# The first wave's four base rows: turned on TensorE, or turned in blocks on VectorE and carried inside SBUF

## What is computed

```
# layer 0, per batch
q, k, v = x @ Wq, x @ Wk, x @ Wv
attn_out = softmax(q k^T / 16) v @ Wp + bp
cms_out  = gelu(attn_out @ cW1 + cb1) @ cW2 + cb2 + one_hot(code)
modifier = gelu(concat(attn_out, cms_out) @ mW1 + mb1) @ mW2 + mb2
x = clip(x + cms_out + modifier, 0, 1)
# layers 1 to 3: adapters, whose weights are picked per batch by role (3 roles)
h = gelu(x @ W_down[role] + b_down[role])
y = x + h @ W_up[role] + b_up[role]
x = (y - mean(y)) * rsqrt(var(y) + 1e-5) * gamma[role] + beta[role]
```

## Time and profile before

| | |
|---|---|
| median of three runs | 352.44 us (352.42 to 353.86) |
| the profiled execution, its own time | 354.08 us |
| its span, first to last instruction | 352.3 us |
| TensorE busy | 341.1 us (97%) |
| VectorE busy | 206.5 us (59%) |
| ScalarE busy | 167.3 us (47%) |
| GpSimd busy | 61.4 us (17%) |
| wave 1's base rows by TensorE (L1569) | four pairs, at 111.9, 115.8, 119.7 and 124.7 us |

### The profile page before, as it was taken

How to read it: one execution, slowest core, us unless ns; L and a number is a source line. 1 busy time by engine, 2 the same in 40 slices (tenths; PEclk the granted TensorE clock), 3 DMA queues, 4 the chain that set the end, 5 groups by cost and what they waited for, 6 DMA issues and landing times.

```text
span 352.3 us, 6682 instructions
## 1 busy us (share of the span) xinstructions
PE 341.1 (97%) x2247; PEld 284.1 (81%) x2247; DVE 206.5 (59%) x493; ACT 167.3 (47%) x331; POOL 61.4 (17%) x96
## 2 busy tenths in 40 slices
PE   6899999999999999999999999999999999999994
PEld 6687687787788888788877777877899999999972
DVE  6048367441452886576554666554689777554576
ACT  3455686463552563544145455343455554543431
POOL 2710060000040110011320111003212125100222
PEclk9899999999999999999999999999999999999998
DMA  6574599468120214234075897303746533288001
GB/s 214 175 254 137 152 139 125 68 139 181 43 60 0 70 39 134 75 90 120 21 245 148 254 309 253 76 31 92 215 151 195 160 113 98 63 281 337 25 2 45
DMA packets 35704, 46.93 MB, mean 133 GB/s; under 512 B 9852, under 2 KB 20406, under 8 KB 35670
## 3 DMA queue, kind: packets, MB, share of 16 engines
q1 hardware_dynamic: 33910, 42.51, 44.9%
q0 software_dynamic: 1392, 3.80, 3.8%
q10 hardware_dynamic: 368, 0.20, 0.2%
HBM read 43.60 MB, written 4.48 MB: 136 GB/s over the span
## 4 chain that ended last, share of the span: by engine, by line
PE 83%; DVE 6%; POOL 3%; ACT 3%; issue 3%; DMA 1%; DVEq 0%; POOLq 0%
PE bank L332 12%; PE bank L334 11%; PE bank L333 11%; PE bank L1499 9%; PE bank L1504 8%; PE bank L1500 8%; PE bank L1546 4%; PE bank L1522 4%; PE bank L1361 2%; PE bank L1403 2%; PE bank L1421 2%; ACT h_full L847 1%; PE bank L1577 1%; ACT h_hi L851 1%; PE bank L1519 1%
## 5 line engine op out<-in xcount | busy, mean ns | idle before, releaser
L847 ACT ACTIVATE h_full<-bank,bias 128x512 f32<-128x512 f32 (+1 forms) x80 | 48.2, 602 | 111.4 <-PE bank L334 101.7
L1082 DVE TENSOR_TENSOR h_lo<-h_full,h_hi 128x512 fp32r<-128x512 f32 (+1 forms) x80 | 46.8, 585 | 60.8 <-ACT h_hi L851 57.4
L767 POOL TENSOR_TENSOR rstd<-moments,minus_half 128x1 f32<-128x1 f32 x39 | 23.4, 600 | 168.6 <-DVE moments L1155 168.5
L851 ACT ACTIVATE h_hi<-h_full 128x512 fp32r<-128x512 f32 (+1 forms) x80 | 43.7, 546 | 2.5
L1140 DVE TENSOR_TENSOR window_y<-bank,window_x 128x256 f32<-128x256 f32 x39 | 16.5, 423 | 37.6 <-PE bank L1522 26.0
L1499 PE MATMUL bank<-h_hi,m_hi 128*128 128x512 f32 (+1 forms) x80 | 30.2, 387 | 0.2
L1499 PE MATMUL bank<-h_hi,c_hi 128*128 128x512 f32 (+1 forms) x80 | 30.1, 385 | 0.2
L332 PE MATMUL bank<-at_hi,c_hi 128*128 128x512 f32 (+1 forms) x80 | 29.3, 367 | 0.0
L332 PE MATMUL bank<-at_hi,m_hi 128*128 128x512 f32 (+1 forms) x80 | 28.7, 359 | 0.0
L334 PE MATMUL bank<-at_lo,c_hi 128*128 128x512 f32 (+1 forms) x80 | 27.8, 348 | 0.0
L333 PE MATMUL bank<-at_hi,c_lo 128*128 128x512 f32 (+1 forms) x80 | 27.8, 347 | 0.0
(11 more groups left out here) (238 smaller groups left out, 729.6 us busy)
## 6 DMA issues: line engine op xcount, KB each, us to landing
adapter_w<-packed_w SPq DMA_DIRECT2D x44, 256.5 KB, 3.4
adapter_rows<-packed_rows SPq DMA_DIRECT2D x36, 256.0 KB, 5.4
stage<-in_L_cond_mW SPq DMA_DIRECT2D x6, 512.0 KB, 4.4
mixed_w<-packed_w SPq DMA_DIRECT2D x8, 256.5 KB, 4.3
stage<-in_L_cond_cW SPq DMA_DIRECT2D x4, 512.0 KB, 5.7
last_w<-packed_w SPq DMA_DIRECT2D x2, 769.5 KB, 6.0
up_bias<-in_L_cond_b_up SPq DMA_DIRECT2D x12, 128.0 KB, 3.7
adapter_rows<-packed_rows SPq DMA_DIRECT2D x24, 64.0 KB
```

The lines of the kernel that those rows point to most:

```text
L767: pool.tensor_tensor(slot.rstd[:, :], slot.moments[:, 1:2], minus_half[:, :], ALU.pow)\
L847: act.activation(h_full[:, n % 2, rows], bank[n % 2][:, rows], ACT.Gelu, bias=bias[:, b:b + 1])\
L851: act.activation(h_hi[:, n % 2, rows], h_full[:, n % 2, rows], ACT.Copy).then_inc(h_hi_ready, 1)
L1082: dve.tensor_tensor(h_lo[:, n % 2, rows], h_full[:, n % 2, rows], h_hi[:, n % 2, rows].bitcast(F32), ALU.subtract).then_inc(h_lo_ready, 1)
```

## The change

Windows 0 to 3 have no "S" use any more: TensorE's eight transposes and VectorE's four additions out of bank 6 go. In their place VectorE turns the 32 x 32 blocks of the window's part of `xT` into `slot.y` (four instructions, windows 0 and 1 behind step H 1 of group 1, windows 2 and 3 behind H 2), SyncE carries them with four transfers for each window from `slot.y` to `slot.x` (sixteen, behind the weights of window 1's layer 1), and VectorE adds `up_bias` to `slot.x` in place, ahead of the addition at L1140. `move_blocks` counts `blocks_turned` four higher, and `row_loads` counts Q = 4 transfers more.

```diff
@@ use numbers of the banks
-                                       [("S", w, 0) for w in starts(wave, spot)] +
+                                       [("S", w, 0) for w in starts(wave, spot) if w not in WAVES[1]] +
@@ row_loads
-            return sum((WIN if v in MIXED else 1) * (2 if n == 0 else 1) for v in range(w % SLOTS, w + 1, SLOTS)
-                       for n in range(LAYERS) if v < w or n <= layer)
+            return Q + sum((WIN if v in MIXED else 1) * (2 if n == 0 else 1) for v in range(w % SLOTS, w + 1, SLOTS)
+                           for n in range(LAYERS) if v < w or n <= layer)
@@ SyncE
-                sp.wait_ge(blocks_turned, n + 1)
+                sp.wait_ge(blocks_turned, len(WAVES[1]) + n + 1)
...
+            def base_rows(w):
+
+                slot = slot_of(w)
+                sp.wait_ge(blocks_turned, w + 1)
+                for m in range(Q):
+                    sp.dma_start(slot.x[:, :].rearrange("p (k m a) -> p m k a", k=VB, m=Q)[:, m, :, :],
+                                 slot.y[quarter(m), :].rearrange("p (i n) -> p i n", i=Q)).then_inc(slot.rows_in, 16)
...
                 window_weights(w, layer)
+                if n == len(WAVES[1]) + 1:
+                    for base in WAVES[1]:
+                        base_rows(base)
@@ VectorE, before: ups
+                    if layer == 0 and w in WAVES[1]:
+                        dve.wait_ge(slot.rows_in, 16 * row_loads(w, 0))
+                        dve.tensor_tensor(slot.x[:, :], slot.x[:, :], slot.up_bias[:, :], ALU.add).then_inc(base_summed, 1)
                     dve.wait_ge(filled[6], use["U", w, layer] + 1)
-                    if layer == 0:
+                    if layer == 0 and w in WAVES[1]:
+                        dve.wait_ge(base_summed, w + 1)
+                    elif layer == 0:
@@ VectorE, after: starts
                 for w in starts(wave, spot):
+                    if w in WAVES[1]:
+                        continue
...
+            def base_blocks(w):
+
+                dve.wait_ge(x1_ready, x1_needed(w))
+                dve.transpose(slot_of(w).y[:, :].rearrange("p (i k a) -> p k i a", i=Q, k=VB),
+                              xT[:, :, columns(w)].rearrange("p k (r i) -> p k i r", i=Q)).then_inc(blocks_turned, 1)
...
+                if g == 1 and step in (("H", 1), ("H", 2)):
+                    for w in WAVES[1][2 * step[1] - 2:2 * step[1]]:
+                        base_blocks(w)
```

More of the change, by code:

```diff
@@ L322, in build @@
         blocks_turned = sem("blocks_turned")
+        base_summed = sem("base_summed")
         blocks_in = [sem(f"blocks_in{n}") for n in range(RING)]
```

## The result

| | before | after |
|---|---|---|
| median, 22 runs each | 352.38 us (352.05 to 353.96, and one of 421.18) | 351.13 us (350.44 to 352.9) |
| ratio to before, 95% interval | | 0.9968 (0.9956 to 0.9981) |
| the profiled execution, its own time | 354.08 us | 350.76 us |
| its span | 352.3 us | 349.0 us |
| TensorE busy | 341.1 us | 337.5 us |

The account below looks back on a forecast made before the run. TensorE was taken as the bound; 0.88 us for transposes plus 0.29 for the bank wait made 1.17 us, off the median 352.44 - 1.17 = 351.3 us. Range 350.3 to 353.2 us, likeliest answer "same".

Parts of the forecast that it names:

- both terms of the sum: Group 1: TensorE's transposes removed, 0.88 us, plus the wait for bank 6 removed, 0.29 us; together 1.17 us.
- What bounds the kernel: Whole kernel: TensorE, busy 341.1 of 352.3 us, with its clock at the upper level in every slice.
- TensorE's transposes: D to H boundaries of group 1: four pairs go, 0.22 us each by distance of starts, 0.88 us gained.
- The shared bank: "Up" matmuls of windows 1 and 2 no longer wait for VectorE to empty bank 6: 0.29 us gained.
- VectorE at nothing: Group 1: VectorE works 2.4 us longer, hidden in idle time and its lead; costs 0, up to 0.1 us.
- The transfers at nothing: SyncE's sixteen transfers, 0.65 us per issue, land 2.5 us or more before the additions want them; cost 0.
- One sign: Profile after, ahead of VectorE's additions: no wait for `rows_in`; a wait for a transfer would prove the forecast wrong.
- Rival 1: After the stage, perhaps SyncE's loads for the mixed windows: the gain doesn't last, 352.4 us; chance 9%.
- Rival 2: TensorE's transposes are worth their durations and the bank wait goes: 2.47 us gained, 350.0 us; chance 8%.
- Rival 3: SyncE's transfers become the bound, window 3 hit first, waiting from 1.29 us per issue; slower, 359.0 us; chance 5%.
- c: Time for one issue of SyncE's sixteen transfers, taken as 0.65 us, with ends 0.38 and 1.40.
- Rival 4: VectorE's order, additions ahead of the "up" wait, costs small waits of some tenths: 351.5 to 352.2 us; chance 4%.

Follow-up runs that it names:

- e1: Kernel before, with the base rows of windows 0 to 2 turned into bank 7 instead of bank 6, transposes kept: stage 25.47 us, 0.27 less than before.
- e5: Changed kernel with VectorE's four block transposes one step later, behind H 2 and H 3: stage 24.78 us, 0.29 more than after.
- e7: e4 once more, on another chip: stage 24.00 us, 351.17 us where before had 353.06, ratio 0.9949.
- e9: e4 once more, on one chip beside the changed kernel: stage 23.98 us, 350.87 us, ratio to before 0.9967.
- e2: Changed kernel with TensorE's eight transposes put back as work nobody reads: stage 25.45 us, 0.96 more than after.
- e4: Changed kernel with layer 1 of windows 0 and 1 also moved by VectorE and SyncE: stage 23.99 us, median 350.82 us, ratio to before 0.9954.

## Why the prediction was right

The mechanism was right, and both terms of the sum were measured by themselves. That the time came within 0.1 us of the forecast is in part luck, since the interval of the measured gain is 0.7 to 1.5 us; the stage alone, 1.25 us in the traces, is the firmer number.

- **What bounds the kernel.** One reading was wrong: I wrote that the clock is at the upper level in every slice, but the earlier trace rows has an 8 in the second. That is the fall from 15.8 to 19 us. It lies ahead of the stage and changes no term; that the profiled execution lies 1.6 us above the median was taken into the forecast without its cause.
- **TensorE's transposes**, 4 x 0.22 = 0.88 us. Put back without a reader they cost 0.96, so a pair is 0.24 with what it shifts behind it. The choice of distances over durations was the step that decided; the durations, 2.18, would have missed by more than a microsecond.
- **The shared bank**, 0.29 us read from the chain: 0.27 by e1.
- **VectorE at nothing.** The places were right (two pairs of transposes, both in idle time). VectorE's busy time rose by 1.9 us where 2.4 was taken. A transpose from `xT` took 0.606 us where 0.63 was taken, an addition within SBUF 0.42 where 0.4 was. What I said of its lead was too wide: for h_lo it is 3 to 4 us (the h_lo that is made at 112.94 to 113.63 is read at 116.78), but for the bank's emptying e5 shows some 1.1 us at window 1. The conclusion held because the transposes were not put there.
- **The transfers at nothing.** Issue 0.614 us and 11.13 us for sixteen, 0.70 each where 0.65 was taken, with one issue of 1.12 among them; landing 2.0 where 1.9 was. Window 3 was in at 115.7 + 2.0 = 117.7 us, more than 6 us before it is read at 123.80. One sign was wrong: I wrote that VectorE would not wait for a transfer at all, and it waits 0.62 us for window 0, since it reaches the addition early and has nothing else to do. The wait ends 2.2 us before the next thing it needs, so it costs nothing; the sign to look for was a wait that ends last.
- **Rival 1**, a gain that doesn't last: from the stage's end to the span's end are 221.1 us before and 221.0 after, and 220.9 to 221.2 in the traces of e1 to e5 and e7 to e9. Out.
- **Rival 2**, durations: out by e2.
- **Rival 3**, transfers as the bound: not this kernel. With the transfers cut in two (c = 1.39) the stage is 1.88 us longer where its sum gives 1.5, and 1.31 of it by the very wait that was named (window 3's sum, the "up" of window 0, layer 1). Two things in it were off: from the landing to the "up" are 129.15 - 128.02 = 1.13 us where 0.9 was taken, and windows 1 and 2 were hit ahead of window 3. Where the waiting begins is shown only to lie between c = 0.70 and 1.39. The rule of the Trainium skill ("VectorE: DVE Perf Modes", the three transpose paths) that a plain transfer must not do the transposing doesn't reach this case, which the trace shows: with the elements turned by VectorE and runs of 128 bytes, an issue takes 0.61 us and lands in 2.0.
- **Rival 4**, small waits of VectorE's order: none in the chain of after.

## What to carry to other kernels

Price an instruction on the bound engine by the distance between its neighbours' starts with and without it, not by its row's duration: here these were 0.11 and 0.27 us for the same transpose. When a step leaves the bound engine, look also for the buffer that it shared, since its wait goes too (about a fifth of this gain). A chain of small transfers is free as long as its last landing, and the work that the consumer does on it, lie before the next use; for pieces of 128 and 256 bytes the number to watch was the issues, not the bytes or the pieces.

## What the runs showed of the hardware

**The issue of a small transfer inside SBUF took about the same time for half and for double the pieces or bytes.** 128 pieces of 128 bytes took 0.603 us, 256 pieces 0.614, and 128 pieces of 256 bytes 0.597. These three shapes are all that was measured, and loads of other shapes differ (0.379 us for L561). In seven of the nine traces with the new transfers the longest issue of the chain took 1.1 to 1.4 us, in the other two 0.76 and 0.83.

**The granted clock can fall at the start, and such executions are 1.5 to 2 us longer.** One trace shows it; the others are known by the mean clock. Of the 22 runs after the change 15 took 350.4 to 351.2 us at a mean clock of 0.996 to 1.000, and seven 352.6 to 352.9 at 0.994. On one chip none of 14 runs had it, nine of before and five of e7. Busy time by single microseconds in the profiled execution of before (PE, PEld, DVE, ACT, POOL, clock, DMA share, GB/s): TensorE is at the lower of its two levels from 15.8 us on, behind a stretch in which it waited for the gather.

```profile
13.00:14.00 1.00, 0.24 (x2) 0.13 (x1) 0.18 (x1) 0.68 (x2) 0.75 (x1) 1.00 0.47 143
14.00:15.00 1.00, 0.66 (x4) 0.42 (x4) 0.42 (x2) 0.24 (x1) 0.95 (x1) 1.00 0.47 119
15.00:16.00 1.00, 0.39 (x2) 0.40 (x3) 0.00 (x0) 0.36 (x1) 0.69 (x2) 0.86 0.15 45
16.00:17.00 1.00, 1.00 (x6) 0.91 (x5) 0.00 (x0) 0.32 (x1) 0.70 (x2) 0.50 0.47 116
```

The profiled execution of after, the same microseconds. TensorE did no more there, yet the clock stayed up:

```profile
13.00:14.00 1.00, 0.00 (x0) 0.00 (x0) 0.59 (x2) 0.27 (x2) 0.70 (x2) 1.00 0.53 150
14.00:15.00 1.00, 0.55 (x4) 0.42 (x4) 0.00 (x0) 0.00 (x0) 0.83 (x1) 1.00 0.46 135
15.00:16.00 1.00, 0.62 (x6) 0.52 (x6) 0.00 (x0) 0.60 (x1) 0.86 (x1) 1.00 0.43 98
16.00:17.00 1.00, 1.00 (x7) 0.90 (x6) 0.00 (x0) 0.83 (x2) 0.69 (x2) 1.00 0.59 75
```

One kernel tried to hold the clock by filling this stretch: e4 with thirteen more matmuls that nobody reads, into bank 0 (`keep_busy` takes the bank in this kernel).

```diff
+            keep_busy(10, b=0)
             half_part("X", 0)
+            keep_busy(3, b=0)
             half_part("X", 1)
```

> e4_all_moved with 13 more matmuls that nobody reads on TensorE, near 12 to 15 us, where it waits for the gather of x (10 ahead of the first transposes of xr, 3 ahead of the second). In the profile of before the granted clock fell to 0.50 from 15.8 to 19 us, behind a stretch in which TensorE was busy for 0.24, 0.66 and 0.39 of three single microseconds; in the profile of after it did not. Theory: this fall is what splits the times of every kernel here in two groups 1.7 to 2 us apart (350.8 and 352.8 after the change), and a filled stretch keeps the clock at 1.0: all executions near 350.5. Rival, that the fall doesn't hang on what TensorE does there: the two groups stay, in about the same shares.

Measured: 356.58 us (354.2 to 357.13), ratio to before 1.0106 (1.009 to 1.0121), slower than every other kernel here (e7, the same without the filling, took 351.17 us on the same chip). In its profile (352.4 us span) the clock was at 1.00 in every microsecond from 12 to 21, but TensorE then sat idle, and the start of the folding (L1389) came at 19.5 us where after has 15.97:

```profile
19.52 1.78 PE L1389 MATMUL bank<-xT,fold 128*128 128x256 f32 x7 [2.28 <-issue]
```

The filled matmuls end at 15.7 and 16.8 us by their rows, yet ScalarE began with the first turned half only at 18.87 us. Which of the two is late, the real end of the filled matmuls or the gather, the rows don't tell; and only one of the executions has a trace. And since neither before nor e7 had the fall on this chip, a clock that stays up here proves nothing for the filling. So neither the cause of the fall nor a way around it is shown. What stays is a warning for reading profiles: two executions that differ by 3.3 us can hold a change of 1.25.
